# Two fused adapter layers on one core: the second half's row work moved a tile further ahead, and a quarter of the convolution's products left out

## The reference

```
c0  = mix of the 64 channels of a batch by its own 64x64 matrix (softmax over 8 kernels)
x1  = x + c0 @ W0.T + LoRA0(c0), 8 experts of rank 16, top 2 by a gate
c1  = conv1d over the 1024 positions, 9 taps, 4 groups of 16 channels, + bias
x2  = x1 + c1 @ W1.T + b + LoRA1(c1), weights softmax over 8 experts of sum(q*k)/sqrt(32)
```

## Time and profile before

| | us |
|---|---|
| median of 3 runs | 1398.41 |
| lowest, highest | 1393.86, 1399.07 |
| the profiled execution's own time | 1400.79 |
| its span in the trace | 1399.0 |
| TensorE matmuls busy in the span | 1314.3 (94%) |
| VectorE, ScalarE, GpSimd busy | 817.7, 299.3, 243.2 |

### The profile page before, as it was taken

How to read it: one execution, slowest core, us unless ns; L and a number is a source line. 1 busy time by engine, 2 the same in 40 slices (tenths; PEclk the granted TensorE clock), 3 DMA queues, 4 the chain that set the end, 5 groups by cost and what they waited for, 6 DMA issues and landing times.

```text
span 1399.0 us, 21738 instructions
## 1 busy us (share of the span) xinstructions
PE 1314.3 (94%) x7429; PEld 1205.9 (86%) x7429; DVE 817.7 (58%) x2039; ACT 299.3 (21%) x510; POOL 243.2 (17%) x145
## 2 busy tenths in 40 slices
PE   6699999999999987999999999999999999999998
PEld 6699999999999986878888888888888888888887
DVE  6878888888888885434434434444434544544543
ACT  5422322332232232111111111111111111111111
POOL 4422232222223223200010010010010010010010
PEclk9899999999999999999999999999999999999999
DMA  5423222222322245332332332332332332332330
GB/s 204 154 69 99 70 68 84 86 68 68 102 68 68 88 127 178 101 83 65 98 94 64 98 94 65 90 100 66 96 95 65 89 96 71 85 95 76 88 83 34
DMA packets 100291, 125.68 MB, mean 90 GB/s; under 512 B 5168, under 2 KB 80944, under 8 KB 100272
## 3 DMA queue, kind: packets, MB, share of 16 engines
q1 hardware_dynamic: 100272, 125.43, 31.2%
HBM read 71.62 MB, written 53.80 MB: 90 GB/s over the span
## 4 chain that ended last, share of the span: by engine, by line
PE 49%; DMA 22%; DVE 17%; ACT 5%; issue 4%; DVEq 1%; ACTq 0%; SPq 0%
DMA x_round<-row 13%; PE ps L952 12%; PE ps L954 12%; PE ps L953 12%; DMA z<-x_round 9%; PE ps L1077 5%; PE ps L1078 4%; DVE gate L731 2%; PE ps L995 2%; ACT row L520 2%; DVE row L848 2%; DVE whole L695 2%; DVE part_l L854 2%; ACT part_h L594 1%; DVE whole L698 1%
## 5 line engine op out<-in xcount | busy, mean ns | idle before, releaser
L952 PE MATMUL ps<-weights,lhs_h 128*128 128x396 f32 (+2 forms) x1792 | 633.3, 353 | 14.3 <-DVE row L717 6.3
L953 PE MATMUL ps<-weights,lhs_h 128*128 128x396 f32 (+2 forms) x1792 | 626.0, 349 | 0.0
L954 PE MATMUL ps<-weights,lhs_l 128*128 128x396 f32 (+2 forms) x1792 | 625.6, 349 | 0.0
L952 PEld LDWEIGHTS ps<-weights,lhs_h 128*128 128x128 f32 x1792 | 340.5, 190 | 37.9 <-issue 14.4
L954 PEld LDWEIGHTS ps<-weights,lhs_l 128*128 128x128 f32 x1792 | 339.6, 189 | 21.0
L953 PEld LDWEIGHTS ps<-weights,lhs_h 128*128 128x128 f32 x1792 | 340.0, 190 | 18.5
L483 POOL TENSOR_TENSOR xo<-row,on_all 128x512 f32<-128x512 f32 x64 | 84.0, 1337 | 716.2 <-DVE row L848 716.2
L1077 PE MATMUL ps<-conv_hl,part_h 128*128 128x256 f32 x512 | 127.4, 288 | 42.1 <-DVE part_l L854 42.1
L1077 PEld LDWEIGHTS ps<-conv_hl,part_h 128*128 128x128 f32 x512 | 96.4, 188 | 57.3 <-DVE part_l L854 56.0
L854 DVE TENSOR_TENSOR part_l<-z,part_h 128x516 fp32r<-128x516 f32 x64 | 41.7, 693 | 152.3 <-ACT part_h L594 152.3
L1078 PE MATMUL ps<-conv_hl,part_l 128*128 128x256 f32 x512 | 124.1, 282 | 0.0
(11 more groups left out here) (144 smaller groups left out, 1294.5 us busy)
## 6 DMA issues: line engine op xcount, KB each, us to landing
spill<-row SPq DMA_DIRECT2D x32, 584.5 KB, 3.8
row<-spill SPq DMA_DIRECT2D x31, 584.5 KB, 4.1
z<-x_round SPq DMA_DIRECT2D x32, 516.0 KB, 4.0
xo<-in_x SPq DMA_DIRECT2D x32, 512.0 KB, 4.1
x_round<-row SPq DMA_DIRECT2D x64, 256.0 KB, 5.1
out_x<-xo SPq DMA_DIRECT2D x31, 512.0 KB, 2.9
staging<-in_w SPq DMA_DIRECT2D x8, 832.0 KB, 6.2
bias_in<-cond_rows SPq DMA_DIRECT2D x63, 64.0 KB, 4.1
```

Source lines behind the costliest of these rows:

```text
L952: pe.matmul(out_ap, lhs[0], rhs[0], start=first, stop=False, skip_group_check=True)
L953: pe.matmul(out_ap, lhs[0], rhs[1], start=False, stop=False, skip_group_check=True)
L954: return pe.matmul(out_ap, lhs[1], rhs[0], start=False, stop=last, skip_group_check=True)
```

## The change

Of tile t + 2 and no longer t + 1, `phase_b(t)` now does `tw_turn`, `tw_high`, `tw_low`, `lora_first`, `x1_add`, `x1_store` (the store of the old `x1_to_z`), `z_load` (its load), `z_high` and `z_low`. `gates`, `gate_exp` and the row's load are those of t + 3. GpSimd's work stays as it was but for the number of tiles written out. `conv(t+1, ..)` stands right behind k=1 and inside k=2. Tile 0 does both its old work for tile 1 and the new work for tile 2. The transposed expert weights go to another PSUM bank, and `conv(.., 1)` waits in addition for `x1_add` of the tile after, whose product shares its banks. In `conv` the low part of z is multiplied by the taps' high part alone: the second matmul of each pair has 128 columns in place of 256, and low times low is left out.

```diff
-        def tiles(eng, body, last=TILES):
+        def tiles(eng, body, tail=2):
 
             for t in (0, 1):
                 body(t, t, 0)
-            with eng.Fori(1, last // 2 - 1) as it:
+            with eng.Fori(1, (TILES - tail) // 2) as it:
                 for u in range(2):
                     body(it * 2 + u, u, it)
-            for t in (last - 2, last - 1):
+            for t in range(TILES - tail, TILES):
                 body(t, t % 2, t // 2)
+
+        def tw_bank(t):
+
+            return BQ[2] if isinstance(t, int) and t < 2 else BQ[1]
...
-            def x1_to_z(t, u, it):
-
-                ready = [t * 2 + 1, t * 2 + 2] if isinstance(t, int) else [sp.snap(t * 2 + 1), sp.snap(t * 2 + 2)]
-                out_done = (it + 1) * 32 if isinstance(it, int) else sp.snap((it + 1) * 32)
+            def x1_store(t, u):
+
+                ready = counts(t * 2 + 1, t * 2 + 2)
                 if at(t, 0):
                     sp.wait_ge(padded, 32)
+                if later(t, 1):
+                    split_before, = counts(t * 2)
+                    sp.wait_ge(z_hi, split_before)
+                    sp.wait_ge(z_lo, split_before)
+                    sp.sem_inc(passed_sp, 1)
                 for h in range(2):
                     sp.wait_ge(x1_ready, ready[h])
-                    if h == 0 and later(t, 1):
-                        sp.wait_ge(z_hi, prev[0])
-                        sp.wait_ge(z_lo, prev[0])
-                        sp.sem_inc(passed_sp, 1)
                     w = 1 - h
                     sp.dma_start(half_rows(u, h)[:, :, w:w + P],
                                  row[:, u, Y0 + 512 * h:Y0 + 512 * h + 512].rearrange("p (s i) -> p s i", i=P)
                                  ).then_inc(x1_out[u], 16)
+
+            def z_load(u, it):
+                out_done, = counts((it + 1) * 32)
                 sp.wait_ge(x1_out[u], out_done)
                 sp.sem_inc(passed_sp, 1)
                 sp.dma_start(z[:, :, :], x1_round[u].rearrange("b q w -> q b w")).then_inc(z_in, 16)
...
+            def next_row(t, u, it):
+
+                added, left = counts(t * 2 - 2, it * 32)
+                sp.wait_ge(xb_ready, added)
+                sp.wait_ge(x1_out[u], left)
+                sp.sem_inc(passed_sp, 1)
+                load_row(t, u)
+
+            def next_bias(t, u):
+                read_before, = counts(t * 2 - 2)
+                sp.wait_ge(conv_read, read_before)
+                sp.sem_inc(passed_sp, 1)
+                load_bias(1, t, u)
+
             def phase_b(t, u, it):
-                twice, row_left = counts(t * 2 + 2, (it + 1) * 32)
-                prev[0] = twice
+                if at(t, 0):
+                    next_row(2, 0, 1)
+                    x1_store(1, 1)
+                    z_load(1, 0)
                 if before_end(t, 2):
-                    sp.wait_ge(xb_ready, twice)
-                    sp.wait_ge(x1_out[u], row_left)
-                    sp.sem_inc(passed_sp, 1)
-                    load_row(t + 2, u)
-                    sp.wait_ge(conv_read, twice)
-                    sp.sem_inc(passed_sp, 1)
-                    load_bias(1, t + 2, u)
-                if before_end(t, 1):
-                    x1_to_z(t + 1, 1 - u, it + u)
+                    next_bias(t + 2, u)
+                if before_end(t, 2) and not at(t, 0):
+                    x1_store(t + 2, u)
+                if before_end(t, 3):
+                    next_row(t + 3, 1 - u, it + u + 1)
+                if at(t, 0):
+                    x1_store(2, 0)
+                if before_end(t, 2):
+                    z_load(u, it + 1)
                 if at(t, TILES - 1):
                     for h in range(2):
                         sp.wait_ge(y_read, t * 2 + h + 1)
                         q = slice(512 * h, 512 * h + 512)
                         sp.dma_start(out[bass.ts(t, P), q], xo[:, u, q]).then_inc(last_stored[h], 16)
                     return
+                twice, = counts(t * 2 + 2)
                 sp.wait_ge(y_read, twice)
                 sp.sem_inc(passed_sp, 1)
                 sp.dma_start(out[bass.ts(t, P), :], xo[:, u, :]).then_inc(stored[u], 16)
...
             def phase_b(t, u, it):
-                if before_end(t, 1):
-                    tw_high(t + 1)
-                if at(t, 0):
+                if at(t, 0):
+                    tw_high(1)
                     split_hi(N1 + 7)
+                elif before_end(t, 2):
+                    tw_high(t + 2)
                 q_copy(t)
                 soft_exp(t)
-                if before_end(t, 1):
-                    z_high(t + 1)
-                hw_high(t)
+                if at(t, 0):
+                    z_high(1)
+                    hw_high(0)
+                    gate_exp(2, 0, 1)
                 if before_end(t, 1):
                     conv_high(t + 1, 1 - u)
+                if at(t, 0):
+                    tw_high(2)
+                else:
+                    hw_high(t)
+                if before_end(t, 3):
+                    gate_exp(t + 3, 1 - u, it + u + 1)
                 if before_end(t, 2):
-                    gate_exp(t + 2, u, it + 1)
-
-            tiles(act, phase_b)
+                    z_high(t + 2)
...
             def phase_b(t, u, it):
-                if before_end(t, 1):
-                    tw_low(t + 1)
-                    x1_add(t + 1, 1 - u)
-                if at(t, 0):
+                if at(t, 0):
+                    tw_low(1)
+                    x1_add(1, 1)
                     split_lo(N1 + 7)
+                elif before_end(t, 2):
+                    tw_low(t + 2)
+                    x1_add(t + 2, u)
                 experts(t)
-                if before_end(t, 1):
-                    z_low(t + 1)
-                hw_low(t)
+                if at(t, 0):
+                    z_low(1)
+                    hw_low(0)
+                    gates(2, 0, 1)
                 if before_end(t, 1):
                     conv_read_low(t + 1, 1 - u, it + u)
+                if at(t, 0):
+                    tw_low(2)
+                    x1_add(2, 0)
+                else:
+                    hw_low(t)
+                if before_end(t, 3):
+                    gates(t + 3, 1 - u, it + u + 1)
+                if at(t, 0):
+                    y_out(0, 0)
                 if before_end(t, 2):
-                    gates(t + 2, u, it + 1)
-                y_out(t, u)
-
-            tiles(dve, phase_b)
+                    z_low(t + 2)
+                if not at(t, 0):
+                    y_out(t, u)
...
             def tw_turn(t):
                 pe.wait_ge(tmpw_ready, t + 1)
-                if later(t, 2):
-                    pe.wait_ge(y_read, t * 2 - 3)
-                pe.transpose(ps[:, BQ[2], 0:P], tmpw[:, :, :].rearrange("p e r -> p (e r)"), eye[:, :]).then_inc(tw_t, 1)
+                pe.transpose(ps[:, tw_bank(t), 0:P], tmpw[:, :, :].rearrange("p e r -> p (e r)"), eye[:, :]).then_inc(tw_t, 1)
 
             def lora_first(t):
                 pe.wait_ge(tw_hi, t + 1)
                 pe.wait_ge(tw_lo, t + 1)
                 if later(t, 1):
-                    pe.wait_ge(conv_read, t * 2)
+                    pe.wait_ge(conv_read, t * 2 if isinstance(t, int) and t < 3 else t * 2 - 2)
                 for h in range(2):
                     q = slice(512 * h, 512 * h + 512)
...
             def conv(t, h):
                 pe.wait_ge(z_lo, t * 2 + 1 + h)
+                if h == 1 and later(t, 2) and before_end(t, 1):
+                    pe.wait_ge(x1_ready, t * 2 + 4)
                 for g in range(GRP):
                     b = GRP * h + g
                     dst = ps[:, (BP1, BP0)[h][g // 2], (g % 2) * 256:(g % 2) * 256 + 256]
                     for m in range(2):
                         both = conv_hl[:, m, g, :, :].rearrange("p s n -> p (s n)")
                         pe.matmul(dst, zh[:, b, m:m + P], both, start=(m == 0), stop=False, skip_group_check=True)
-                        mm = pe.matmul(dst, zl[:, b, m:m + P], both, start=False, stop=(m == 1),
-                                       skip_group_check=True)
+                        mm = pe.matmul(dst[:, 0:P], zl[:, b, m:m + P], conv_hl[:, m, g, 0, :], start=False,
+                                       stop=(m == 1), skip_group_check=True)
                 mm.then_inc(conv_done, 1)
...
+                    pe.wait_ge(tw_lo, 2)
+                    second(0, 0, 2, 0, 7)
                 else:
                     second(t, u, 0, 0, 4)
+                    if before_end(t, 2):
+                        tw_turn(t + 2)
+                    second(t, u, 0, 4, 8, q_done)
+                    if before_end(t, 2):
+                        lora_first(t + 2)
+                    second(t, u, 1, 0, 8, k_done)
                     if nxt:
-                        tw_turn(t + 1)
-                    second(t, u, 0, 4, 8, q_done)
+                        conv(t + 1, 0)
```

(96 more changed lines are left out.)

1 line of the change is left out of this document (removed).

## The result

| | before | changed |
|---|---|---|
| median | 1397.95 us (4 runs, 1393.86 to 1399.07) | 1358.1 us (4 runs, 1354.03 to 1360.99) |
| profiled execution, span | 1400.79, 1399.0 | 1357.82, 1356.0 |

The ratio is 0.9718, with a 95% interval of 0.9686 to 0.9750. The forecast was 1358 us in a range of 1346 to 1369.

The account below looks back on a forecast made before the run. TensorE, busy 95.98 of 100 us, was taken to set the time. The span 1399.0 - 50.2 + 9.9 = 1358.7 us, plus 1.8 beyond the span, gives 1360.5; times 0.9983, 1358 us, range 1346 to 1369.

Parts of the forecast that it names:

- The wait in the steady tiles: TensorE's pause for `z_low` before `conv(t+1, 0)` goes, 0.99 + 0.11 us a tile: 25.88 to 24.78 us.
- The layout of the other engines: Times from a steady tile's start: z's load issued at 11.04 us, `z_high(t+2)` at about 17.7, `z_low(t+2)` done by about 21.3.
- The cover of about 10 us: In steady tiles z may come some 10 us later than 15.1 us into the tile before it costs anything.
- Low times low: 16 convolution matmuls a tile fall from 256 to 128 columns: 0.009 us a pair, 0.15 us a tile.
- the mix's pairs: First half's mix: six matmul pairs of 256 and 128 columns take 1.37 us, 0.228 a pair.
- the 128 x 128 weights: Each convolution matmul needs its own weight load, which hides the rest of the column saving; a pair takes at least 0.213 us.
- Tiles 0 and 1: TensorE waits 8.6 us before `lora_first(3)`, with `tw_high(3)` behind `z_high(2)` on ScalarE; loss 9.9 us, paid once.
- the 0.7 us for GpSimd's hold on VectorE: Tile 1: allowance for GpSimd's x1 + b of tile 2 delaying VectorE before `lora_first(3)`; up to 2.56 us possible.
- z's chain: From `x1_add(2)` to `z_high(2)`, through stores, z's load and ScalarE: 11.12 us, taken from tile 0.
- 21.0 + 1.6: After tile 1's wait: 21.0 us for the rest of the tile, 1.6 us for running at half clock.
- Tiles 2 to 30: 28 tiles of 24.63 us plus tile 30 at 23.2 sum to 712.8 us, where 762.96 was taken: gain 50.2.
- the factor of 0.9983: Whole kernel: the runs' median of 1398.41 us against the profiled execution's 1400.79, applied to 1360.5 us.

Follow-up runs that it names:

- one load more: Changed kernel with z's load made twice in each tile, one after the other: 1373.62 us, ratio 0.9793.
- three more: Changed kernel with z's load made four times in each tile, one after the other: 1515.37 us in one run.
- the kernel with the lead alone: Changed kernel with the convolution's low times low product back in, 256 columns in both matmuls of a pair: 1361.63 us, ratio 0.9727.

## Why the prediction was right, step by step

- *The wait in the steady tiles*: right in place and size. 24.63 us was worked out and 24.64 measured. The layout of the other engines held within 0.1 us for `z_high` and 0.5 us for `z_low`; only z's load came 0.8 us later than laid out. The cover of about 10 us is bracketed, not measured: one load more (4 us) costs a steady tile nothing, three more (12.3 by the times of issue) cost 4.4 us.
- *Low times low*: the size was right (0.15 worked out, 0.145 by the tiles of the kernel with the lead alone), because it was read from the mix's pairs and not from columns. The reason given with it, the 128 x 128 weights, is neither shown nor refuted. The Trainium skill's load time ("TensorE: Matmul & The Clock Gate", section "LDWEIGHTS (loading the stationary operand)") gives an estimate of 107 ns for 128 columns and 53 ns for 64; the traces agree so far that the shorter load is 0.053 us shorter (0.138 against 0.191) and that the step which the first load could set is 0.108. But a fixed least time of that size would show the same.
- *Tiles 0 and 1*: right in mechanism. From tile 0's convolution to tile 2's start it was 35.12 us before and is 619.97 - 576.01 = 43.96, so the loss was 8.8, not 9.9. TensorE stood 7.5 us (from start to start, less one matmul) and not 8.6: the 0.7 us for GpSimd's hold on VectorE wasn't paid (it was GpSimd that took 3.07 us in place of 2.56 beside `z_low`), and z's chain took 10.78 from `x1_add`, not 11.12. From the end of the wait to tile 2's start it took 22.9 us, where 21.0 + 1.6 was worked out.
- *Tiles 2 to 30*: 1333.16 - 619.97 = 713.2 us against 712.8.
- *What the sum left out*: tile 0's convolution began at 576.01, 2.0 us earlier than before, though next to nothing ahead of it had changed. The kernel before, profiled again, has it at 573.83. So what lies ahead of it varies by 4 us between executions. For the profiled execution the forecast was 1360.5 us, and it took 1357.82; the factor of 0.9983 that then took 2.3 us off came from one slow execution of the kernel before, and the changed kernel's profiled execution lay at its own median. So the match to 0.1 us is luck; the working itself came within 3 us.

## What to carry to other kernels

A wait that recurs in every tile is bought off by starting its chain a tile earlier; then look at what each in-order queue does in the first tile, where the later step of the next tile stands ahead of an earlier step of this one: here that place alone cost 7 us, and moving two calls gave them back. Read the price of a smaller matmul from a row of the same shapes in the same kernel, not from its columns: from 256 to 128 columns the pair gave 0.009 us, from 128 to 32 nothing. To learn what an instruction costs, shorten one that nothing else covers. A saving on TensorE inside a tile that waits can be lost to its clock; remove the wait first.

## What the runs showed of the hardware that was not expected

- A pair of matmuls with a load each, the first of 256 columns, took 0.228 us with 128 or 32 columns in the second, and with 128 or 64 columns of weights in the second load. Its loads start 0.108 and 0.120 us apart by turns; with 256 columns in both matmuls it is 0.119 and 0.117.
- With the convolution's second matmul at 128 columns behind a wait of 1 to 2 us, nine of 58 tiles in two executions had a granted clock of 0.94 or less and took about 2 us more; with 256 columns it was one of 58. Over all executions the mean granted clock was 0.986 (12) against 0.989 (17).
